# Masks and decay spreads of a hybrid block: bf16 parts on TensorE, the causal mask by GpSimd selects

## The reference, cut to what matters

```python
x = x + deltanet(layernorm(x), ...)          # x: (8, 512, 128)
x = x + layernorm(x) @ sign(W_ffn).T
x = x + attention(layernorm(x), ...)
x = x + layernorm(x) @ sign(W_ffn).T

# deltanet, per head h (8 of width 16) and stream j (2):
beta_eff = minimum(sigmoid(beta_t) * r, 0.9999)
S = S * beta_eff + g_t * outer(k_t, v_t);  z = z * beta_eff + g_t * k_t
y_t = sum_j softmax(mix)_j * (q_t @ S) / (q_t @ z + 1e-6)

# attention, 16 heads of width 8, rotary positions:
scores = einsum('bhsd,bhtd->bhst', q, k) * scale
scores = where(causal, finfo.min, scores)      # causal: t > s
ctx = einsum('bhst,bhtd->bhsd', softmax(scores), v)
```

## Time and profile before

| | us |
|---|---|
| median of 3 runs | 784.66 (783.12 to 786.89) |
| profiled execution | 781.32 |
| its span, first to last instruction | 779.4 |
| PE busy | 687.1 (88%) |
| DVE busy | 566.8 (73%) |
| ACT busy | 420.7 (54%) |
| POOL busy | 190.3 (24%) |

### The profile page before, as it was taken

One profiled execution on the slowest core, in us unless ns is written; L12 is line 12 of the kernel. 1 busy time (PEld: TensorE's weight loads), 2 busy tenths in 40 slices (PEclk: granted clock), 3 DMA queues, 4 the chain that ended last, 5 costly groups with the idle time before them and its releaser, 6 DMA issues.

```text
span 779.4 us, 17611 instructions
## 1 busy us (share of the span) xinstructions
PE 687.1 (88%) x6737; PEld 394.5 (51%) x6768; DVE 566.8 (73%) x1579; ACT 420.7 (54%) x884; POOL 190.3 (24%) x231
## 2 busy tenths in 40 slices
PE   3676877789999999999999999999999988987885
PEld 2444535445555666565656555646564544434323
DVE  5675773788977979898889778987898778457302
ACT  2534452445676568556855567466846553452561
POOL 4241441244033302431323224221223100001000
PEclk9689696799999999999999999999999999699986
DMA  3000017000450144005400450044005302330000
GB/s 103 0 2 1 15 47 117 0 16 3 86 93 2 39 80 77 1 10 105 82 2 24 85 87 2 9 102 71 2 16 104 63 8 50 54 57 16 16 1 15
DMA packets 20646, 32.38 MB, mean 42 GB/s; under 512 B 3017, under 2 KB 17993, under 8 KB 18249
## 3 DMA queue, kind: packets, MB, share of 16 engines
q1 hardware_dynamic: 20562, 31.25, 21.0%
HBM read 22.46 MB, written 8.39 MB: 40 GB/s over the span
## 4 chain that ended last, share of the span: by engine, by line
PE 63%; DVE 18%; DMA 6%; ACT 6%; issue 4%; SPq 1%; POOL 0%; DVEq 0%; ACTq 0%; POOLq 0%
PE ps L983 9%; PE ps L1023 9%; PE ps L1008 7%; DVE mrow L1452 6%; PE ps L772 5%; PE ps L965 4%; DMA ks<-scratch 4%; PE ps L843 3%; PE ps L985 3%; PE ps L870 3%; PE ps L819 3%; PE ps L1010 3%; PE ps L767 2%; DVE am L1300 2%; PE ps L890 2%
## 5 line engine op out<-in xcount | busy, mean ns | idle before, releaser
L1452 DVE TENSOR_REDUCE mrow<-ps 128x1 f32<-128x384 f32 (+3 forms) x352 | 224.1, 637 | 100.2 <-PE ps L985 97.6
L738 ACT ACTIVATE pT<-ps 128x512 f32<-128x512 f32 (+1 forms) x352 | 187.9, 557 | 130.2 <-PE ps L1010 127.2
L983 PE MATMUL ps<-ks,qs 72*128 72x512 bf16 (+3 forms) x512 | 142.7, 311 | 23.7 <-DVE mrow L1452 18.4
L1008 PE MATMUL ps<-qs,ks 75*128 75x256 bf16 (+3 forms) x512 | 134.2, 309 | 2.7 <-ACT pT L738 1.8
L983 PEld LDWEIGHTS ps<-ks,qs 72*128 72x128 bf16 x512 | 50.0, 98 | 109.3 <-DVE mrow L1452 84.5
L985 PE MATMUL ps<-cbf 128*128 128x128 bf16 x512 | 101.7, 224 | 0.0
L1023 PE MATMUL ps<-pT,va 128*32 128x512 f32 (+3 forms) x1024 | 98.9, 462 | 3.0 <-ACT pT L738 2.8
L1010 PE MATMUL ps<-cbf 128*128 128x128 bf16 x512 | 99.5, 224 | 0.0
L532 POOL TENSOR_TENSOR spread<-state,cst 128x144 f32<-128x144 f32 x112 | 48.6, 455 | 180.4 <-DVE state L1329 143.6
L1008 PEld LDWEIGHTS ps<-qs,ks 75*128 75x128 bf16 x512 | 50.9, 100 | 70.2 <-ACT pT L738 29.9
L520 POOL TENSOR_TENSOR xe<-lpart,hot 96x1024 bf16<-96x1024 bf16 x32 | 61.0, 1909 | 56.2 <-DVE lpart L1276 56.2
(11 more groups left out here) (194 smaller groups left out, 1134.7 us busy)
## 6 DMA issues: line engine op xcount, KB each, us to landing
ks<-scratch SPq DMA_DIRECT2D x48, 192.0 KB
scratch<-parts SPq DMA_DIRECT2D x48, 128.0 KB, 2.3
qs<-scratch SPq DMA_DIRECT2D x32, 128.0 KB
qs<-scratch SPq DMA_DIRECT2D x16, 192.0 KB
x<-x SPq DMA_DIRECT2D x8, 256.0 KB, 3.1
qs<-scratch SPq DMA_DIRECT2D x32, 64.0 KB
out<-xk SPq DMA_DIRECT2D x8, 256.0 KB, 2.4
qs<-mT SPq DMA_DIRECT2D x48, 8.0 KB
```

Source lines behind the costliest of these rows:

```text
L738: act.activation(pT[:, c0:c0 + m, P_OFF[kt]:P_OFF[kt] + width], ps[:, BK_SC[n % 2], 0:m * width].rearrange("p (m n) -> p m n", n=width), A ...
L983: pe.matmul(o, qs[0:K_MAX, f % RING, h, qt * P:(qt + 1) * P], ks[0:K_MAX, f % RING, h, 0:width], start=True, stop=False, skip_group_check= ...
L1008: pe.matmul(o, ks[0:K_ALL, place, h, kt * P:(kt + 1) * P], qs[0:K_ALL, place, h, kt * P:T], start=True, stop=False, skip_group_check=True)
L1452: dve.tensor_reduce(mrow[:, qt, h0:h0 + m], ps[:, BK_MAX, 0:m * width].rearrange("p (m k) -> p m k", k=width), AX.X, ALU.max).then_inc(max ...
```

## The change

In scan, `lrow` goes away. `sel` becomes a bf16 matrix of 96 rows, and the decays are spread from the three bf16 parts `lpart` directly: the 96-row product adds the parts up again. The `lown` rows are made by the scalar engine with a per-partition scale, after the copy of the keys, and no longer by VectorE. In attn, the mask matmul is dropped. GpSimd gets 16 new steps a batch: an AFFINE_SELECT over the diagonal tile of the 4 heads in `pT` (128 x 4 x 128), in place, which keeps queries not before the key and writes 0 elsewhere. The values step waits for the select (`probs_cut`) instead of the exponentials. The mask matmuls of maxima stay. The tables of letters are new for all engines.

```diff
 ACT_ORDER = (
-    "nsssssssssssssssssssssssssssnmmsmsmsssssssssssssmsssssmmssssmsmmmssssnsmsssssssssssssssssssmssssxasaasas"
+    "nsssssssssssssssssssssnssssmsssmsmsmssssssssmsssssssssssmmsssssmmmmssssnsssssmsssssssssssssssmsssssxasaa"
...
-        sel = sb("sel", [QUAD, NQ, J, D])
+        sel = sb("sel", [PARTS * QUAD, NQ, J, D], BF16)
...
-        lrow = sb("lrow", [QUAD, C, LB])
...
             def attn(b):
+                for n in range(16):
+                    yield
+                    g, kt = n // 4, n % 4
+                    last = max(k for k, e in enumerate(EXP_GROUPS) if e[0] == kt)
+                    pool.wait_ge(probs_ready, b * 4 * NE + g * NE + last + 1)
+                    diagonal = pT[:, :, P_OFF[kt]:P_OFF[kt] + P]
+                    pool.affine_select(diagonal, diagonal, [[0, 4], [1, P]], ALU.is_ge, 0.0, base=0,
+                                       channel_multiplier=-1).then_inc(probs_cut, 1)
                 yield
                 rsqrt(var_attn, b + 1, an, rstd_attn)
...
                 if b > 0:
                     act.wait_ge(xe_ready, b * 4)
                     act.wait_ge(lown_ready, b)
+                    act.wait_ge(pre_ps, b * 2)
...
                 act.activation(ktok[:, :, :], token_bank(BK_E), ACT.Copy).then_inc(ktok_ready, 1)
-
+                yield
+                act.wait_ge(lpart2, b + 1)
+                if b == 0:
+                    act.wait_ge(scan_set, 1)
+                else:
+                    act.wait_ge(e_ps, b * 8)
+                for q in range(NQ):
+                    ins = act.activation(lown[used, :, q, :], lpart[used, :, :], ACT.Copy, scale=rowm[used, 3 + q:4 + q])
+                ins.then_inc(lown_ready, 1)
...
                     if cp == 0:
-                        pe.wait_ge(l_ready, b + 1)
+                        pe.wait_ge(lpart2, b + 1)
...
-                            mm = pe.matmul(o[:, :, j, q, :], sel[:, q, j, :], lrow[:, 2 * cp:2 * cp + 2, :],
+                            mm = pe.matmul(o[:, :, j, q, :], sel[:, q, j, :], lpart[0:PARTS * QUAD, 2 * cp:2 * cp + 2, :],
                                            start=True, stop=True)
...
-                        o = ps[:, BK_SC[n % 2], i * width:(i + 1) * width]
-                        pe.matmul(o, ks[0:K_ALL, place, h, kt * P:(kt + 1) * P], qs[0:K_ALL, place, h, kt * P:T],
-                                  start=True, stop=False, skip_group_check=True)
-                        mm = pe.matmul(o[:, 0:P], ident_bf, future_kq, start=False, stop=True, skip_group_check=True)
+                        mm = pe.matmul(ps[:, BK_SC[n % 2], i * width:(i + 1) * width],
+                                       ks[0:K_ALL, place, h, kt * P:(kt + 1) * P], qs[0:K_ALL, place, h, kt * P:T],
+                                       start=True, stop=True)
                     mm.then_inc(sc_ps, 1)
 
                 def values(g, kt):
-                    last = max(k for k, e in enumerate(EXP_GROUPS) if e[0] == kt)
-                    pe.wait_ge(probs_ready, b * 4 * NE + g * NE + last + 1)
+                    pe.wait_ge(probs_cut, b * 16 + g * 4 + kt + 1)
...
-                    cols = ident[0:QUAD, HJ * q:HJ * q + HJ].rearrange("p (h j) -> p j h", j=J)
-                    dve.tensor_copy(sel[:, q, :, :].rearrange("p j (h d) -> p j h d", d=DH),
-                                    cols.unsqueeze(3).broadcast_to([QUAD, J, H, DH]))
...
+                cols = midT[used, D:D + HJ].rearrange("p (h j) -> p j h", j=J)
+                for q in range(NQ):
+                    dve.tensor_scalar(sel[:, q, :, :].rearrange("p j (h d) -> p j h d", d=DH),
+                                      cols.unsqueeze(3).broadcast_to([PARTS * QUAD, J, H, DH]), rowm[used, q:q + 1], None,
+                                      ALU.mult)
...
-                if b > 0:
-                    dve.wait_ge(pre_ps, b * 2)
-                dve.tensor_copy(lrow[:, :, :], decays[0:QUAD]).then_inc(l_ready, 1)
-                yield
                 dve.wait_ge(lpart1, b + 1)
                 dve.tensor_tensor(lpart[third, :, :], lres[third, :, :], lpart[third, :, :], ALU.subtract).then_inc(lpart2, 1)
-                yield
-                dve.wait_ge(lpart2, b + 1)
-                if b == 0:
-                    dve.wait_ge(scan_set, 1)
-                else:
-                    dve.wait_ge(e_ps, b * 8)
-                used = slice(0, PARTS * QUAD)
-                for q in range(NQ):
-                    ins = dve.tensor_scalar(lown[used, :, q, :], lpart[used, :, :], rowm[used, 3 + q:4 + q], None, ALU.mult)
-                ins.then_inc(lown_ready, 1)
```

72 lines of the change are left out of this document (37 added, 35 removed).

## The result

The changed kernel takes 803.12 us, the median of 4 runs (799.31 to 805.39); the kernel before took 783.89 (4 runs, 782.64 to 786.89). The ratio is 1.0235, with a 95% interval of 1.0184 to 1.0285. The forecast was 773 us, faster; it is slower, by 18 us by the ratio (14 to 22 by its interval). The profiled execution took 803.85 us.

The account below looks back on a forecast made before the run. TensorE's amount of work was taken to bound the middle, latency the end. Lead -5, middle -18, 620 to 740 us +4, end +7 sum to -12 us, from the 784.7 us median to 773 us; range 753 to 806.

Parts of the forecast that it names:

- What bounds the middle: 200 to 620 us: TensorE's work sets the time; 60% of 30.2 us removed work counted, -18 us.
- End, +6.6: From 740 us on: 8 values steps wait for selects, 7.6 us, less 1 us of masks, +6.6 us.
- 620 to 740, +4: 620 to 740 us: bare select waits counted at 10 us, less 6 us for removed masks, net +4 us.
- Select at 1.05 us: GpSimd's 128 selects: 1.05 us each, between a memset's 0.56 and a two-input add's 1.295 us.
- New order: Written order on TensorE: 3.7 other steps ahead of each values step, covering the 1.1 us select delay for TensorE.
- Decays and small moves: bf16 decay groups save 9.4 us of TensorE in the middle; lown goes to the scalar engine at 0.38 us each.
- the lead's -5: Lead, batches 0 to 2: cheaper decay groups on the chain save about 5 us, bounds 2 and 8.
- Attention becomes the bound: Rival, whole run: select waits make attention's in-order steps the bound, slower, 803 us; chance 0.26.
- Nothing left: Rival, middle: the waits take back all of the middle's gain, 784 us; chance 0.11.
- The shared port: Rival, middle: selects hold VectorE's instructions, making VectorE the bound, about +10 us, 795 us; chance 0.06.

Follow-up runs that it names:

- e8: Changed kernel plus 4 unread filler matmuls of 384 columns per values step of the last batch's groups 1 to 3; 799.00 us, ratio 1.0216.
- e12: Kernel before without attention mask matmuls or selects, plus fillers in the last two batches and closing steps; 788.11 us, ratio 1.0104.
- e2: Changed kernel in its own order without its selects, values waiting for the exponentials; 801.15 us, ratio 1.020.
- e1: Kernel before in its own order without the attention's mask matmuls, nothing in their place; 786.17 us, ratio 1.0026.
- e19: Kernel before in its old order with the new decays, without mask matmuls or selects; 791.01 us, ratio 1.0092.
- e21: Kernel before without attention mask matmuls or selects, plus fillers in the last batch and closing steps only; 784.21 us, ratio 1.0026.
- e11: Kernel before, masks kept, plus fillers in the last two batches and closing steps; 789.88 us, ratio 1.0109.
- e17: Kernel before, masks kept, plus fewer fillers, in the last batch only (2 per values step of groups 1 to 3, 3 per closing step); 779.64 us, ratio 0.995.
- e7: Kernel before with its decays and old order, selects replacing the mask matmuls and placed by hand in GpSimd's order; 853.93 us, ratio 1.092.
- e5: Kernel before in its old order with its masks, only the decays' part of the change added; 785.41 us, ratio 1.0035.
- e15: Kernel before with each of the attention's mask matmuls issued twice; 799.78 us, ratio 1.0203.

## Why the prediction was wrong, point by point

- **What bounds the middle** (the step that failed). "TensorE's amount of work sets the middle" was read from 411.8 busy of 420 us. TensorE's recorded work did fall (411.8 to 391.3, 20.5 us, where I had priced 30.2), and I counted 60% of 30.2 us, -18. Measured: -0.8 in the changed kernel, -3 to -7 for the masks alone, +1 to +2 for the decays alone, +6 for both in the old order. "With VectorE at 84% behind it" was the warning, and I took the share of busy time as if the two engines could overlap freely. They talk once per maxima step. TensorE already waited 40.4 us for that between 200 and 620 us, which I gave no term in the middle's sum; it is 49.3 in the changed kernel and 51 to 54 in the three without masks. All its waits for other engines and DMAs in that stretch, added up, went from 83.0 to 102.5 us in the changed kernel: 19.5 more, about what was taken off it.
- **End, +6.6.** It measured +9.9 behind the last maximum. Right in kind, for half the reason. Of the 11 values steps behind the last maximum 8 have a bare select behind the exponential in the chain, 0.65 us and a hop of 0.05 each, 5.6 us in all. I had counted 8 steps and 7.6 us for them (start, us, what):

```profile
755.78 0.63 ACT pT L756
756.47 0.65 POOL pT L570
757.16 1.94 PE ps L1039 x8
...
761.04 0.50 ACT pT L756
761.60 0.65 POOL pT L570
762.29 1.51 PE ps L1039 x8
```

  At full or nearly full clock (0.92 and 1.00) the end takes 44.0 us with selects (e8) and 39.0 without (e12), and at 0.50, in the new order both, 52.0 and 46.8 (e2): 5 us for the selects either way. The other half, 3.6 to 3.7 us (e1 and e19 against before), goes with the clock, 0.58 in place of 0.78 there, which I had only as "some 3" in one rival. In the changed kernel it is 0.50 throughout, and the step of 8 products takes 1.94 us where before had 1.06 at 754.52.
- **620 to 740, +4.** Batch 6 alone got 7.0 us longer, the start of batch 7 3.2 more. The masks' removal gives 1 to 4 of it (e21, e1), hardly more than the scatter, without any select; the rest is the new order with its selects, not separated further.
- **Select at 1.05 us.** It measured 0.634 (median of 128; 629 to 727 ns), near the lower bound of 0.56. The neighbour I chose, a two-input add, was the wrong one: a select reads one tensor. The Trainium skill (GPSIMD Engine Reference, section Engine selection) has one-input operations at roughly line rate: by it I had estimated 0.43 us before dispatch, and the measured 0.634 lies between that and the 1.05 that I took, nearer to the 0.43.
- **New order.** I priced it only as cover. It was good cover, and a cost of its own: about 8 us with the same instructions (e2 against e19). TensorE also waits 4.0 us for `xe` in it where it had waited 0.8; without the selects (e2) it is 3.9, so that is the order's.
- **Decays and small moves.** The product takes 219 ns recorded, so a group costs little, as priced; the lead's -5 did not come: first output +3.1 (before, e11 and e17, with the same code there, gave 266.6 to 268.0), with the third part of lpart at 31.90 us where it was at 29.13, 2.5 us of it because the last constants landed at 12.1 us in that execution and at 9.6 in the one of before. That is no effect of the change: over the profiles of this study they landed anywhere between 9.0 and 12.1 us. lown takes 0.50 us, not 0.38. kd is free of its 2.12 us, as said.

```profile
31.49 0.41 DVE L1290 TENSOR_TENSOR lpart<-lres,lpart 32x256 bf16<-32x256 f32 x1 [0.48 <-ACT lpart L648]
31.94 0.91 ACT L661 ACTIVATE lown<-lpart,rowm 96x256 bf16<-96x256 bf16 x2
...
31.96 1.03 PE L837 MATMUL ps<-lpart,sel 96*128 96x128 bf16 x8 [0.96 <-DVE lpart L1290]
31.98 3.75 POOL L520 TENSOR_TENSOR xe<-lpart,hot 96x1024 bf16<-96x1024 bf16 x2 [1.43 <-DVE lpart L1290]
```

- **The rivals.** *Attention becomes the bound* named 803 us, the time that came, by another mechanism: its 1.1 us waits would have shown as far more than 16.4 us on TensorE (3.7 of it in the middle), and its middle batches as longer. Taking every select away gave 2 to 3 us, not 22. That 803 us lies in my range is therefore luck. (It was also added to the profiled 781.3; added to the median, as the others were, +22 is 807.) Its mechanism may be at work in the old order (e7). The middle went as in *Nothing left*, but I had priced that rival at 784 us: with nothing for the middle my own terms give 784.7 - 5 + 0 + 4 + 7, 791 us. *The shared port* is excluded as the bound: VectorE is less busy, 553.0 us in place of 566.8 in the whole run, and kd takes 424 ns.

By the ratios the loss of 2.35% splits into 0.9% for the two removals, 1.1% for the new order and 0.35% for the selects, each with some 0.4 to 1% of uncertainty; the end's 5 us for the selects, 0.6%, is inside that. Left open: why the two removals together cost where each alone does not (the granted clock is a candidate that no run tried: in steps of 20 us between 200 and 620 us it is below 0.95 in seven of e19's 21, in none of e1's, though in one and two of the other profiles with its code, and in one of e5's), and how much of batch 6 is the order's and how much the clock's (fillers there disturb more than they show).

## What to carry to other kernels

An engine that is recorded as 98% busy still need not repay work taken from it: look at its waits for the runner-up, and try the slope both ways, since doubling a suspected cost and removing it can give different answers. In a tail of short round trips, matmuls that look like waste may hold the clock; a few unread ones in its gaps, and only there, can be worth more than the ones removed. A table that sets the order belongs to one set of durations: judge a change in the old order and in the new one, and never the table and the change together only.

## What the runs showed that was not expected

- The granted clock behind the last maximum was 0.89 with the masks issued twice (e15), 0.78 with them (before), 0.58 without (e1, e19), 0.50 in the new order without them, with selects or not (after, e2), and 1.00 with 2 to 4 fillers ahead of each step (e17, e12): the mean over stretches at the 1.2 and the 2.4 GHz level. With twice the masks the end was shorter than with them once, 39.6 us against 42.1, in one profile each; the row of e15:

```profile
755.00:794.00 39.00, 30.10 (x261) 16.30 (x258) 4.76 (x20) 17.52 (x34) 1.02 (x1) 0.89 0.01 2
```

- The stretch took 39.0 us at 1.00 and 45.7 at 0.58 in kernels that differ in fillers alone.
- GpSimd's affine select over 128 x 512 fp32, in place, takes 0.634 us; its two-input add of the same shape took about twice that, 1.295 us.
- Fillers gained 4 us in the last batch (e17, 2 or 3 ahead of a step) and, one batch earlier, went with a batch 6 that was 4.8 to 6.5 us longer (e11, 4 ahead of a step, 70.9 us against 66.1 and 64.4).
